# Chunked state-space block with MLP and experts: masked products in one group behind v's turn, both output products ahead of exponents 2 and 3

## The reference

```
h = embed(tokens) * sqrt(192) + positions
u = rmsnorm(layernorm(h))
z, xBC, dt = split(u @ in_proj);  xBC = silu(causal_conv4(xBC));  dt = softplus(dt + bias)
per head (24 heads of 16 channels, state 64):
    state = exp(dt * A) * state + dt * x (outer) B ;   y = state . C + D * x
m = (y * silu(z)) @ out_proj
v = rmsnorm(m);   h = h + m + (silu(v @ w_gate) * (v @ w_up)) @ w_down
x = layernorm(h); h = h + (routed 2 of 8 experts + one shared expert)(x)
```

## Time and profile before

| | |
|---|---|
| time, median of 3 runs | 806.73 us (805.35 to 806.88) |
| the profiled execution | 805.65 us, span of its instructions 803.5 us |
| TensorE busy | 767.3 us, 95% of the span |
| VectorE busy | 643.7 us, 80% |
| ScalarE busy | 549.0 us, 68% |
| GpSimd busy | 284.5 us, 35% |
| mean granted clock of TensorE | 0.992 |
| chain that ended last | 86% TensorE |

### The profile page before, as it was taken

The page is one execution under the profiler, slowest core; times in us unless marked ns, Lnnn a source line. Parts: engine busy times, 40 slices in busy tenths (PEclk is TensorE's granted clock), DMA queues, the critical chain, the costliest instruction groups (busy, mean ns, idle before and its releaser), DMA issues.

```text
span 803.5 us, 23139 instructions
## 1 busy us (share of the span) xinstructions
PE 767.3 (95%) x7374; PEld 655.2 (82%) x7374; DVE 643.7 (80%) x1712; ACT 549.0 (68%) x1228; POOL 284.5 (35%) x427
## 2 busy tenths in 40 slices
PE   3679999999999999999999999999999999999897
PEld 2447888888888888888888888888888888888786
DVE  5699987879788787978878797887889788786745
ACT  4975776767677676767767676776767777676533
POOL 2254342423434242343324234332423433242122
PEclk9899999999999999999999999999999999999999
DMA  7410010000000000000000000000000000000000
GB/s 244 164 66 2 1 26 2 7 19 6 18 0 24 0 6 18 6 18 0 24 0 6 18 3 21 0 21 3 6 18 3 21 0 17 7 6 11 3 1 20
DMA packets 13475, 16.77 MB, mean 21 GB/s; under 512 B 1986, under 2 KB 12104, under 8 KB 13000
## 3 DMA queue, kind: packets, MB, share of 16 engines
q1 hardware_dynamic: 13448, 16.43, 6.4%
HBM read 12.23 MB, written 4.19 MB: 20 GB/s over the span
## 4 chain that ended last, share of the span: by engine, by line
PE 86%; DVE 3%; issue 1%; ACT 1%; POOL 0%; POOLq 0%; DVEq 0%; ACTq 0%
PE bank L1540 39%; PE bank L1932 11%; PE bank L1859 8%; PE bank L1715 5%; PE bank L1704 5%; PE bank L1828 4%; PE bank L1815 3%; PE bank L1806 2%; PE bank L1792 2%; PE bank L1644 1%; DVE mr L1176 1%; PE bank L1568 1%; PE bank L1649 1%; PE bank L1688 1%; PE bank L1899 1%
## 5 line engine op out<-in xcount | busy, mean ns | idle before, releaser
L1176 DVE SCALAR_TENSOR_TENSOR mr<-er,gm 128x512 f32<-128x512 f32 x192 | 126.0, 692 | 5.2 <-ACT er L753 3.5
L753 ACT ACTIVATE er<-bank 128x512 f32<-128x512 f32 x192 | 106.0, 596 | 18.3 <-PE bank L1704 17.7
L1932 PE MATMUL bank<-w2t,w_raw 128*128 128x192 f32 x576 | 112.6, 327 | 0.4 <-DVE w_raw L1345 0.4
L843 ACT ACTIVATE sg<-bank 128x256 f32<-128x256 f32 x144 | 55.1, 383 | 62.3 <-PE bank L1540 51.4
L1115 DVE SCALAR_TENSOR_TENSOR xa<-xr,cw_,xa 128x256 f32<-128x256 f32 x192 | 92.4, 488 | 6.1 <-ACT xa L661 4.5
L1932 PEld LDWEIGHTS bank<-w2t,w_raw 128*128 128x128 f32 x576 | 91.0, 190 | 1.8 <-DVE w_raw L1438 0.7
L792 ACT ACTIVATE sg<-bank 128x256 f32<-128x256 f32 x90 | 34.3, 381 | 65.5 <-PE bank L1540 46.4
L1540 PE MATMUL bank<-x_h,w_hi 128*128 128x256 f16 x288 | 78.6, 273 | 0.0
L1540 PE MATMUL bank<-x_h,wt_lo 128*128 128x256 f16 x288 | 78.7, 273 | 0.0
L1540 PE MATMUL bank<-x_h,w_lo 128*128 128x256 f16 x288 | 78.6, 273 | 0.0
L1540 PE MATMUL bank<-x_l,w_hi 128*128 128x256 f16 x288 | 78.6, 273 | 0.0
(11 more groups left out here) (244 smaller groups left out, 2162.1 us busy)
## 6 DMA issues: line engine op xcount, KB each, us to landing
out<-w_raw SPq DMA_DIRECT2D x16, 192.0 KB, 2.0
pos<-position SPq DMA_DIRECT2D x16, 96.0 KB, 2.9
ri<-exponent_rows SPq DMA_DIRECT2D x1, 1536.0 KB, 6.4
w_raw<-weights SPq DMA_DIRECT2D x1, 1156.0 KB, 5.5
wt_raw<-weights SPq DMA_DIRECT2D x1, 1156.0 KB, 8.8
tok<-tokens SPq DMA_DIRECT2D x16, 70.0 KB
sums<-lj SPq DMA_DIRECT2D x16, 64.0 KB, 1.9
w2t<-w SPq DMA_DIRECT2D x1, 864.0 KB, 11.3
```

The costliest lines, as they stand in the source:

```text
L753: act.activation(er[:, r % NER], p_d[r % 2][:].rearrange("p (h i) -> p h i", h=HG), ACT.Exp)\
L843: act.activation(sg[:, e % 4, :], src[e][:, 0:NB * Q], ACT.Silu).then_inc(sx_ready, 1)
L1176: ve.scalar_tensor_tensor(mr[:, r % NMR], er[:, r % NER], 1.0, gm[:, r // NQ, :].unsqueeze(1).to_broadcast([128, HG, Q]), ALU.min, ALU.mult)\
L1932: ins = pe.matmul(p_ex[e][:, b * D:(b + 1) * D], hh[:, e % NHH, b * Q:(b + 1) * Q], w2t[:, e, :], start=True, stop=True)
```

## The change

On TensorE both output products come one after the other, ahead of exponents 2 and 3 instead of around exponents 2. The first sequence's masked products, four units ahead of v's turn and two behind exponents 7, become one group of six units behind exponents 7; v's turn comes right behind exponents 5. ScalarE takes the squares of the norm ahead of exponential 2 instead of 3, and writes v_t ahead of exponential 4 instead of 5. VectorE takes `from_state` and `v_low` after four masks instead of five. The same is done in the loop's body and in the finale. No instruction is added or removed.

```
# ScalarE, body and finale
-exponentials(f, range(6), {3: lambda: mixed(b), 5: lambda: mixed_norm(b)})
+exponentials(f, range(6), {2: lambda: mixed(b), 4: lambda: mixed_norm(b)})
# VectorE, body and finale
-masks(f, range(5))
+masks(f, range(4))
 from_state(f, 0)
 v_low(b)
-masks(f, (5,))
+masks(f, (4, 5))
# TensorE, scan_front
 state_read(c, 0, None)
 exponents(c, 5)
-masked(c, range(4))
+turned(lambda: state_share(c, 0))
 exponents(c, 6)
-turned(lambda: state_share(c, 0))
 exponents(c, 7)
-masked(c, (4, 5))
+masked(c, range(NQ))
# TensorE, body and finale
 exponents(b, 0)
 exponents(b, 1)
 project_out(a, 0)
+project_out(a, 1)
 exponents(b, 2)
-project_out(a, 1)
 exponents(b, 3)
 scan_front(b, lambda shared: turn_v(a, between=shared))
```

More of the change, by code:

```diff
@@ L869, in finale @@
             def finale(a, b):
-                exponentials(b, range(6), {3: lambda: mixed(a), 5: lambda: mixed_norm(a)})
+                exponentials(b, range(6), {2: lambda: mixed(a), 4: lambda: mixed_norm(a)})
                 split_v(a)
@@ L1375, in finale @@
             def finale(a, b):
-                masks(b, range(5))
+                masks(b, range(4))
                 from_state(b, 0)
                 v_low(a)
-                masks(b, (5,))
+                masks(b, (4, 5))
                 split_v(a)
@@ L2103, in body @@
                 project_out(b, 0)
+                project_out(b, 1)
                 if f is not None:
                     exponents(f, 2)
-                project_out(b, 1)
-                if f is not None:
                     exponents(f, 3)
```

## The result

The changed kernel takes 825.1 us (median of 4 runs, 824.8 to 825.6), the kernel before beside it 806.49; the ratio is 1.0235 (95% interval 1.0222 to 1.0248). Ratios here come from the single runs, so they can differ by 0.0005 from the quotient of the medians. The prediction said 826, between 816 and 835.

A forecast was written before the change was run, and what follows sets the result against it. TensorE's in-order queue, without waits behind the front, was taken as the bound. Per chunk +1.41 -0.07 +0.35 -0.27 = 1.42 us; 14 x 1.42 + 0.2 = 20.1 on 805.65, stated as 826 us, range 816 to 835.

The forecast's parts named there:

- Steps 1 and 2: Front, TensorE: second output product starts at 395.73, its result comes 0.22 us earlier; exponents 4 reached at 397.14 as before.
- Step 3: Front: exponents 4 waits 1.41 us (1.35 to 1.55) for exponential 2, which stands behind the squares on ScalarE.
- Steps 4 and 5: Front: exponents 5 loses its 0.07 us wait; in v's turn the state share waits 0.57 for t, against 0.22.
- Step 6: Front, after v's turn: exponents 6 and 7 run at 401.95 and 402.16 without a wait.
- Step 7: Front: one masked x48 group of 1.47 us instead of 1.64, one switch of 0.1 saved: gain 0.27 per chunk.
- Step 8: End of front: the MLP's first product at 403.94 against 402.52, so a chunk grows by 1.42 us (1.1 to 1.8).
- The first front: Front ahead of the loop: the new wait replaces 1.25 us of waiting for VectorE's masks; only 0.2 us counted.
- The finale: Last of the 15 fronts: counted among the 14 that each grow by 1.42 us.
- the falling clock: Rival: each new wait is followed by 3.40 us at half speed, costing some 1.7 us; 843 us; chance 0.08.
- The rival that the delay is absorbed: Rest of the chunk takes up the delay: wholly, so not slower (800 us, chance 0.04), or in part (816, chance 0.06).

The follow-up runs named there:

- e6: Kernel before with only ScalarE's squares of the norm moved ahead of exponential 2 instead of 3: 825.0 us, ratio 1.0234.
- e7: Kernel before with only both output products put ahead of exponents 2 on TensorE: 813.1 us, ratio 1.0089.
- e2: Kernel before with only TensorE's scan front changed (turn behind exponents 5, one masked group of six units): 820.1 us, ratio 1.0175.
- e3: Changed kernel with the old scan front, so only output products, ScalarE's and VectorE's orders are changed: 822.3 us, ratio 1.0193.
- e1: Changed kernel with ScalarE's old order back (squares ahead of exponential 3, v_t ahead of exponential 5): 820.8 us, ratio 1.0174.
- e4: Changed kernel with skip terms and state read moved ahead of exponents 4 on TensorE: 817.6 us, ratio 1.0143.
- e8: Changed kernel with TensorE and VectorE reordered so that work not needing exponential 2 fills the time in which it is made: 802.3 us, ratio 0.9949.
- e5: Kernel before with only VectorE's new order (t and v_low behind four masks instead of five): 805.1 us, ratio 0.9984.

## Why the prediction was right

- Steps 1 and 2 (output products together, TensorE at exponents 4 just where it stood): the products take 406.72 - 404.73 = 1.99, as forecast.
- Step 3 (the new wait): 1.43 against 1.41, and e6 shows its cause, the squares ahead of exponential 2. e7 adds a correction: with the squares left behind, exponents 4 waits 0.72 only.
- Steps 4 and 5 (exponents 5 without a wait, the share waiting for t): 0.53 against 0.57.
- Step 6: exponents 6 and 7 run without a wait, as forecast.
- Step 7 (one group of x48): 413.94 - 412.47 = 1.47 as in the earlier trace rows. e2 has the same group. (The last mask was put at 402.8 and "a third" into the group; by the prediction's own times it is 0.33 of 1.47, nearer a quarter. Nothing hangs on it.) That the group does not pay was right in the sum, but the prediction told it as a gain of 0.27 beside the losses. e2 shows that the same move costs 1.06 where exponents 4 doesn't wait: it takes away the filling ahead of v's turn. In the changed kernel most of that cost hides behind the wait at exponents 4, which gives v_t time to come; 0.31 of it stays, as e3 shows.
- Step 8: the front is 9.72, the forecast 403.94 - 394.21 = 9.73. The period grows by 1.37 instead of 1.42, as 0.04 us or so of small waits behind the front went.
- The first front: forecast +0.2. The front itself is 0.5 longer, but its chunk as a whole 0.35 shorter. The prediction had the MLP's own waits at nothing in every chunk. In this one TensorE waits for VectorE's `gt`, the gated product of the MLP, and in the changed kernel, where it gets there later, `gt` is ready or nearly so. Before:

```profile
75.39 0.28 PE L1540 MATMUL bank<-v_h,w_hi 128*128 128x256 f16 x1 [0.22 <-DVE gt L1222]
...
77.91 0.28 PE L1540 MATMUL bank<-v_h,w_hi 128*128 128x256 f16 x1 [0.60 <-DVE gt L1222]
```

 In the changed kernel the first of these waits is gone and the second is 0.14. Counted from the MLP's first product, TensorE is 0.84 us earlier behind them: 0.5 less 0.84 is the measured -0.35, but for 0.01.
- The finale: forecast +1.42 like the others, measured +0.4. Its front is 1.48 longer. About 0.45 came back at a wait for `gt` in its MLP (0.28 before, none after). Another 0.6 came back behind its second sequence's masked products, where this execution kept full clock:

```profile
764.50:767.90 3.40, 2.00 (x15) 1.43 (x13) 2.74 (x7) 2.02 (x4) 1.01 (x2) 1.00 0.03 7
767.90:771.30 3.40, 2.20 (x52) 1.68 (x52) 3.11 (x8) 1.93 (x3) 0.19 (x1) 1.00 0.01 2
```

 These are stretches of the changed kernel around the wait for the second norm, the columns as in the earlier trace rows; in the earlier trace rows the stretch from 749.20 had 0.50. These 0.6 us can't be put down to the change: executions of several kernels show the one or the other, and the single runs of the kernel before have mean granted clocks from 0.989 to 0.993.
- Among the rivals, the falling clock didn't come (granted clock 1.00 in all loop chunks). The rival that the delay is absorbed was wrong for the 13 loop chunks and right in part for the first and the last. The row that the prediction leaned on for a short wait without a fall, 42.12 in the earlier trace rows, doesn't show the clock behind it; this stretch of the kernel before does:

```profile
42.80:46.20 3.40, 3.17 (x25) 1.85 (x25) 3.27 (x7) 3.39 (x6) 2.52 (x8) 1.00 0.04 13
```

So 14 x 1.42 + 0.2 = 20.1 stands against 17.9 - 0.35 + 0.4 = 17.9 without the ramp; the medians differ by 18.6. Of the 2.2 too much, 1.0 is the finale, 0.6 the first chunk and 0.6 the loop (13 x 1.42 = 18.5 against 17.9). That 826 comes so near to 825.1 is in part luck: the sum stood on the profiled execution's 805.65, and on the median of 806.73 it is 826.8. The ends of the range mix the two as well: 821 is 805.65 + 15.4, but 832 is 806.73 + 25.7.

## What to carry to other kernels

In a queue that runs in order, moving a piece of work forward can cost more than it brings: e6 moves one line on an engine that then sits idle 1.4 us and loses 18.6 us of 806, because the moved work waits for something late, and everything behind it waits with it. Groups of the same work are worth joining only if their pieces were not the filling ahead of some other engine's result: here the join itself wins 0.17 to 0.27 us, and the chunk still comes out 1.06 longer (e2). When several chains stand close together, single repairs give back a part only (e1, e4), and halves of a loss don't add up; lay out all chains through the stretch with the latencies of the trace, and order the queue so that each wait is covered (e8).

## What was not expected of the hardware

The wait of 2.0 us for the second norm stands in the finale of every kernel here. In some executions (before, e1, e5, e8) the granted clock then fell to 0.50, 1.2 GHz, for one stretch of 3.4 us; in others (the change, e2, e3, e4, e6, e7) it didn't. The masked products behind that wait, first before and then in the changed kernel, with the wait that follows in the latter:

```profile
748.67 2.38 PE L1715 MATMUL bank<-mr,xd 128*32 128x128 f32 x48
```

```profile
769.22 1.54 PE L1715 MATMUL bank<-mr,xd 128*32 128x128 f32 x48
...
771.62 0.17 PE L1540 MATMUL bank<-w_hi,x_h 128*128 128x8 f16 x1 [0.86 <-DVE x_h L1046]
```

Between the masked products and the next output products lie 754.13 - 748.67 = 5.46 us with the fall and 774.05 - 769.22 = 4.83 us without, the same work. So the fall cost 0.63 us there, and not the 1.7 that the prediction put on one: at full clock TensorE gets to the next products early and waits 0.86 for VectorE's `x_h`, at half clock it doesn't. By these numbers the work itself took some 0.63 + 0.86 = 1.5 us longer, an estimate. What decides between the two wasn't tried. In the changed kernel, e3 and e6 exponents 4 waits 1.4 to 1.6 us once in each of the 13 loop chunks, and that never brought the clock down there.
